# A two-norm block with a sorted mixture of experts on one core: norm sums in order of arrival, a rearranged last block, tie steps at half steps, and six units gathered ahead

## The chip, the cores and the metric

The kernel runs on one core of one Trainium2 chip. The metric is the device time of one execution in microseconds (us). Engines are named as in the profile: PE (TensorE), DVE (VectorE), ACT (ScalarE), POOL (GpSimd) and SP (SyncE, which only issues DMAs here). PEld is TensorE's weight load.

## What is computed

x has 2 sequences of 2048 rows of 128 channels (4096 rows in all). Six modulation vectors per sequence come from silu(c) @ wmod; ga and gb are kept away from zero.

```python
h = layernorm(x) * (1 + ca) + sa
x = x + ga * prefix_mean(h)            # row t gets the mean of rows 0..t of its sequence
h = layernorm(x) * (1 + cb) + sb
x = x + gb * ffn(h)
def ffn(h):                            # 8 experts, hidden width 512
    scores = softmax(h @ gate.T).T     # 8 x 4096
    vals, idx = top_k(scores.reshape(-1), 8192)   # over all experts and rows together
    out = sum over the chosen (expert, row) of val * (gelu(h[row] @ W1[e] + b1[e]) @ W2[e] + b2[e])
    return out + gelu(h @ Ws1 + bs1) @ Ws2 + bs2
```

How many rows an expert gets is known only at run time.

## The kernel before, in words

The rows are cut into NB = 8 blocks of BLK = 512 rows (four tiles of 128 each), and the five engines each run their own hand-written program, held together by counting semaphores. There are three stages.

**Norm stage.** For block j, `stats1(j)` on DVE takes mean and variance of the four tiles of x, `rstd(0, j)` on POOL makes 1/sqrt(var + eps) of it by a power (lines 730 to 741), `norm1(j)` on ACT (two tiles) and DVE (two tiles) normalizes, `turn_x(j)` on PE transposes the normalized tiles (semaphore pe_t1) and x itself (pe_t2), `prefix(j)` on DVE scans along the rows (line 434) and adds (lines 442, 448), `turn_x2(j)` on PE transposes back, `keep_x2(j)` on ACT stores. Then the second norm: `stats2(j)` on DVE, `rstd(1, j)` on POOL, `norm2(j)` on ACT (line 284), `turn_xn2(j)` on PE, `affine2(j)` on ACT (line 292), `logits(j)` (line 855) and `turn_h2(j)` on PE, `rows_out(j)` on ACT, and an SP store of the rows to a scratch tensor in HBM. In DVE's turn j stand norm1(j+1), prefix(j), stats2(j-1), stats1(j+3). In POOL's turn j stand rstd(1, j-1), then rstd(0, j+2). PE's turn j is turn_x(j+1), turn_xn2(j-2), turn_x2(j), logits(j-2), turn_h2(j-2); ACT's is norm1(j+1), norm2(j-2), rows_out(j-3), affine2(j-2), keep_x2(j). `softmax(part)` on DVE with `expo(part)` on ACT turns the logits into scores, part 0 for blocks 0 to 6 and part 1 for block 7.

**Shared stage, steps 0 to 31.** Step s holds `up(s)` (line 892) and `down(s-2)` (line 916) on PE, each 128x512 in float32, with `gelu(s)` on ACT between: the shared expert, four steps a block. `close(b)` (PE transposes, DVE adds X2, line 538, SP stores `out`) ends block b, four steps after its last up. Beside it a search of 30 bits finds the 8192nd largest score, one bit in each half step from half step 3 to 32 (`bit`). Then five tie steps sort out equal scores and make the counts of each expert: `ties(0)` at step 17 (masks), `ties(1)` at 18 (line 554), `ties(2)` at 19, `ties(3)` at 20 (line 570), `ties(4)` at 21 (PE transposes, line 948, then STC, `idx_mask(0)`, the units' experts EIDI, `idx_mm(0)`, `idx_count(0)`). Rows chosen for an expert are cut into units of up to 512 rows; between 16 and 23 units are in use (USED, 18 with this input). The list of rows of a unit comes from `idx_mask(v)` (DVE), `idx_mm(v)` (PE) and `idx_count(v)` (DVE, lines 646 to 655, which ends with IDXB and v_idx). Units 1 and 2 have theirs in steps 22 to 24.

**Unit stage, from step UNIT1 = 32.** Unit v has four steps, c = 0 to 3. PE runs in each step `up` (line 898), then what stands at that c, then `down` of two steps earlier. At c = 1 stand `xt(v+1)` (the transposes of the gathered rows of unit v+1, which wait for its gather to land) and `idx_mm(v+3)`; at c = 3 stands `yt(v-1)` (transposes of the result of unit v-1). So in PE's order yt(u) of unit u stands behind xt(u+2). DVE's `yo(u)` (line 689) scales the rows of yt(u) by their gates into YO, which has two buffers, and POOL scatters them:

```python
# before, POOL, in unit v's step c == 3
if 0 <= v - 1 < NU: scatter(v - 1)      # waits: yo(v-1) done, scatter(v-2) landed
if v + 3 < NU:      gather(v + 3)       # 4 indirect DMAs (line 766)
```

A scatter is four indirect DMAs that add to `out` (line 779). scatter(0) also waits until all of `out` from the shared stage has been stored. Gathers 0, 1 and 2 are issued before the unit stage; gather(3) and scatter(0) follow in it. gather(v) waits for v_idx of its unit, and for a free buffer of XG (XR = 5 of them). Units from UMIN = 16 on stand in a branch that skips them when they are not in use.

Of the kernel before, what the change touches and what calls it, by code (L numbers as in the profile page):

```python
# [32 lines left out]
XR = 5  # L33
# [7 lines left out]
TIE0 = max(BIT_AT) // 2 + 1  # L41
GS0 = NC * NB
UNIT1 = max(GS0, TIE0 + 8)
XT_STEP = UNIT1 - 1 - TIE0
# [3 lines left out]
ld_wu0 ld_wu1 ld_wu2 ld_wu3 ld_xg0 ld_xg1 ld_xg2 ld_xg3 ld_xg4  # L48
# [4 lines left out]
v_cols v_mod v_gbd v_st v_ag1 v_ag2 v_xn v_ct v_mt v_x2 v_sub v_sc v_tk v_cnt v_cand v_mask v_tie v_sel v_out  # L53
# [13 lines left out]
def adaln_moe(nc, x, gw, w1, b1, w2, b2, ws1, bs1, ws2, bs2, c_in, wmod, consts, ucon, icon, inv, out):  # L67
    rows_dram = nc.dram_tensor("rows_scratch", [S + NPAD, ROW], F32, kind="Internal").ap()

    with ExitStack() as ctx:  # L70
# [99 lines left out]
        TOKA = (NB - 1) * NT  # L170
# [12 lines left out]
        def sync(eng):  # L183
# [49 lines left out]
            for s in range(NSTEP):  # L233
                g = on_step(s - LAG - 2)
                if g is not None and g < GS0 and g % NC == NC - 1:
                    b = g // NC
# [4 lines left out]
                if s == TIE0 + 5:  # L241
# [10 lines left out]
        def scalar(eng):  # L252
# [54 lines left out]
            for j in range(NB + 2):  # L307
                if j + 1 < NB:
                    norm1(j + 1)
                if j >= 2:  # L310
                    norm2(j - 2)
                if j == 2:
# [50 lines left out]
            for s in range(NSTEP):  # L363
# [7 lines left out]
                if s == TIE0 + 4:  # L371
# [4 lines left out]
                if s == TIE0 + XT_STEP:  # L376
# [12 lines left out]
        def vector(eng):  # L389
# [33 lines left out]

            def prefix(b):
# [43 lines left out]
            def softmax(part):  # L468
# [3 lines left out]
                logits = LG[:, 0:TOKA * E] if part == 0 else RB[0][:, 0:NT * E]  # L472
# [4 lines left out]
                eng.wait_ge(M["pe_lg"], NB - 1 + part)  # L477
                k = step("v_tk", eng.tensor_reduce(mx, logits, AX_X, ALU.max))
                eng.wait_ge(M["v_tk"], k)
                eng.tensor_tensor(ex, logits, mx.unsqueeze(2).to_broadcast([P, n, E]),  # L480
                                  ALU.subtract).then_inc(M["v_sub"], 1)
# [14 lines left out]
            for j in range(NB):  # L496
# [43 lines left out]
            def ties(s):  # L540
                TF = T_I.bitcast(F32)
                ones = ONES[:, 0:1].to_broadcast([P, 256])
                if s == 0:
# [7 lines left out]
                elif s == 1:  # L551
# [8 lines left out]
                elif s == 2:  # L560
# [5 lines left out]
                elif s == 3:  # L566
# [32 lines left out]
                elif s == 4:  # L599
# [15 lines left out]
                elif s == 5:
                    idx_mask(1)
                elif s == 6:
                    idx_mask(2)
                    idx_count(1)
                elif s == 7:  # L620
                    idx_count(2)
# [70 lines left out]

            eng.wait_ge(M["v_sc"], 2)
            count(0)
            for s in range(NSTEP):
                if 2 * s in BIT_AT:
                    bit(BIT_AT[2 * s])
                g = on_step(s - LAG - 2)
                if g is not None and g < GS0 and g % NC == NC - 1:
                    close(g // NC)  # L700
                if 0 <= s - TIE0 <= XT_STEP:
                    ties(s - TIE0)
                if 2 * s + 1 in BIT_AT:
                    bit(BIT_AT[2 * s + 1])
                if s == TIE0 + XT_STEP:
# [369 lines left out]
```

## Time and profile before

| | us |
|---|---|
| median of 3 timed runs | 405.81 (405.25 to 410.68) |
| the profiled execution | 403.75 |
| its span in the trace | 402.0 |
| busy: PE / DVE / ACT / POOL | 297.1 / 168.1 / 138.1 / 209.7 |
| DMA | 35.96 MB, 89 GB/s on average |

A row of the timeline reads: start, duration, engine, line, operation, what is written <- what is read, shape, and, in brackets, how long the engine had been idle and what it had waited for. Several equal instructions in a row are merged (x4). Line numbers are those of the kernel printed above. R is one of the big SBUF and PSUM tensors whose names begin with R (the gathered rows among them), R1b the PSUM bank of the result transposes, XW holds x and later the experts' weights.

### The profile page before, as it was taken

Reading aid. Unit: us, or ns where it says so; the run is one execution under the profiler, and the core shown is the slowest. Engines: PE = TensorE matmul, PEld = TensorE weight load, DVE = VectorE, ACT = ScalarE, POOL = GpSimd, SP = SyncE. Lnnn points to the kernel's source line nnn. Section 1 sums busy time; section 2 is a strip of 40 time slices with the busy share of each in tenths; the row PEclk is TensorE's granted clock in tenths of the full one; section 3 lists DMA queues with packets and bytes.
Section 4 is the critical chain, followed back from the end, with each engine's and each line's share of the span. In section 5 each row is a group of like instructions: output and inputs, shape, how many; then the busy total and the mean of one; then the engine's idle time right before and its main releaser. Section 6 shows DMA issues by size and latency. Waiting matters only on the chain.

```text
span 402.0 us, 4835 instructions
## 1 busy us (share of the span) xinstructions
PE 297.1 (74%) x1158; PEld 162.7 (40%) x1158; DVE 168.1 (42%) x774; ACT 138.1 (34%) x228; POOL 209.7 (52%) x216
## 2 busy tenths in 40 slices
PE   1647667799999699998776977679786897669500
PEld 1536657653334344544332543335343344234200
DVE  2777748247775860244344213442144323211200
ACT  2135546743334235433233333233232333233200
POOL 2333443100000065037878788787888788786662
PEclk9998665569999999999899889898899989898955
DMA  8907200230000095044455554555445555342331
GB/s 231 294 2 201 62 27 30 68 48 0 27 28 27 26 277 147 28 127 87 76 118 126 105 102 82 115 126 106 100 82 119 125 103 104 74 73 27 30 34 13
DMA packets 49886, 35.96 MB, mean 89 GB/s; under 512 B 7816, under 2 KB 44479, under 8 KB 49855
## 3 DMA queue, kind: packets, MB, share of 16 engines
q0 software_dynamic: 13824, 14.46, 21.1%
q1 hardware_dynamic: 35792, 20.73, 18.5%
q10 hardware_dynamic: 238, 0.42, 0.4%
q8 instruction: 12, 0.20, 0.2%
q14 instruction: 20, 0.16, 0.1%
HBM read 23.65 MB, written 11.94 MB: 89 GB/s over the span
## 4 chain that ended last, share of the span: by engine, by line
POOL 34%; PE 23%; issue 17%; DMA 11%; DVE 11%; ACT 1%; SPq 1%; POOLq 0%; DVEq 0%; ACTq 0%
POOL out_dram L779 23%; POOL R L766 9%; PE Y L916 8%; DMA out_dram<-YO,IDXB 8%; PE U L892 7%; DVE R L434 2%; DMA XW<-in_L_attn_x_dram 2%; DVE ST L400 2%; PE U L898 2%; PE R1b L810 1%; DVE R L442 1%; DVE R L448 1%; PE R L810 1%; PE LG L855 1%; PE LG L922 1%
## 5 line engine op out<-in xcount | busy, mean ns | idle before, releaser
L779 POOL DMA_INDIRECT out_dram<-YO,IDXB x72 | 113.5, 1576 | 31.0 <-issue 20.7
L766 POOL DMA_INDIRECT R<-rows_scratch,IDXB x72 | 69.9, 971 | 105.5 <-DVE IDXB L655 68.9
L335 ACT ACTIVATE HF<-U,CB 128x512 f32<-128x512 f32 x72 | 49.5, 687 | 100.3 <-PE U L898 100.3
L916 PE MATMUL Y<-HF,XW 128*128 128x512 f32 x144 | 83.1, 664 | 0.0
L898 PE MATMUL U<-XT,XW 128*128 128x512 f32 x144 | 78.9, 631 | 0.7 <-issue 0.7
L689 DVE SCALAR_TENSOR_TENSOR YO<-R1b,GT,R 128x128 f32<-128x128 f32 x72 | 20.3, 344 | 122.4 <-PE R1b L810 122.4
L810 PE MATMUL R<-CST,R 128*128 128x128 f32 x104 | 21.5, 343 | 40.6 <-DMA R<-rows_scratch,IDXB 39.9
L898 PEld LDWEIGHTS U<-XT,XW 128*128 128x128 f32 x144 | 29.7, 208 | 39.6 <-issue 39.6
L810 PEld LDWEIGHTS R<-CST,R 128*128 128x128 f32 x104 | 15.0, 173 | 54.7 <-DMA R<-rows_scratch,IDXB 51.5
L892 PE MATMUL U<-H2F,WS 128*128 128x512 f32 x64 | 36.7, 663 | 0.0
L335 ACT ACTIVATE HF<-U,COL 128x512 f32<-128x512 f32 x32 | 22.0, 687 | 42.5 <-PE U L892 42.2
L916 PEld LDWEIGHTS Y<-HF,XW 128*128 128x128 f32 x144 | 27.2, 210 | 21.4 <-issue 21.4
L916 PE MATMUL Y<-HF,WS 128*128 128x512 f32 x64 | 34.7, 624 | 0.0
L735 POOL TENSOR_SCALAR VE<-MV 128x4 f32<-128x4 f32 x16 | 3.1, 194 | 45.2 <-DVE MV L403 44.8
L646 DVE TENSOR_SCALAR_CACHE_REDUCE GJ<-R,UC 128x128 f32<-128x128 f32 x72 | 25.1, 349 | 2.3 <-PE LG L971 0.4
L351 ACT ACTIVATE XT<-R 128x512 f32<-128x512 f32 x18 | 10.7, 595 | 41.9 <-PE R L810 41.9
L810 PE MATMUL U<-CST,R 128*128 128x128 f32 x32 | 8.9, 433 | 17.9 <-ACT R L270 15.8
L968 PE MATMUL R<-DQ,HM 128*128 128x128 f16 x144 | 15.4, 234 | 3.4 <-DVE HM L631 2.8
L738 POOL TENSOR_TENSOR RS<-VE,SM 128x4 f32<-128x4 f32 x16 | 16.2, 1015 | 0.0
L517 DVE TENSOR_SCALAR_CACHE_REDUCE TK<-SCT,TI 128x256 f32<-128x256 f32 x30 | 14.4, 479 | 1.1
L916 PEld LDWEIGHTS Y<-HF,WS 128*128 128x128 f32 x64 | 11.2, 194 | 8.7 <-issue 8.7
L810 PEld LDWEIGHTS U<-CST,R 128*128 128x128 f32 x32 | 5.9, 223 | 20.1 <-ACT R L270 17.7
(136 smaller groups left out, 357.6 us busy)
## 6 DMA issues: line engine op xcount, KB each, us to landing
XW<-in_L_ffn_W_dram SPq DMA_DIRECT2D x36, 256.0 KB, 3.1
XW<-in_L_attn_x_dram SPq DMA_DIRECT2D x8, 256.0 KB, 7.1
rows_scratch<-GBC SPq DMA_DIRECT2D x2, 1024.0 KB, 7.3
rows_scratch<-HT SPq DMA_DIRECT2D x8, 256.0 KB, 2.4
out_dram<-SHO SPq DMA_DIRECT2D x8, 256.0 KB, 2.3
R<-rows_scratch,IDXB POOLq DMA_INDIRECT x72, 2.8
out_dram<-YO,IDXB POOLq DMA_INDIRECT x72, 3.3
INV<-in_inv_dram SPq DMA_DIRECT2D x4, 256.0 KB, 6.4
```

The costliest lines, as they stand in the source:

```text
L335: eng.activation(HF[:, g % RING, :], UB[g % 2][:, :], ACT.Gelu_apprx_tanh, bias=bias).then_inc(M["a_gelu"], 1)
L517: eng.tensor_scalar(GT, SCT[:, :], C_I.bitcast(F32), None, ALU.is_ge, ALU.add, accum_out=CNT[:, i % 2:i % 2 + 1]).then_inc(M["v_cnt"], 1)
L646: eng.tensor_scalar(GJ[:, :], bank[:, s * P:(s + 1) * P], SIG[:, i:i + 1], None, ALU.is_le, ALU.add, accum_out=c0[:, s:s + 1]).then_inc(M[ ...
L689: m = eng.scalar_tensor_tensor(YO[:, k, t, :], RB[1][:, t * P:(t + 1) * P], GT4[:, k, t:t + 1], XG[:, r, t, D + E:ROW], ALU.mult, ALU.mult)
L738: eng.tensor_tensor(RS[:, k, b, 0, :], VE[:, k, b, :], NHALF, ALU.pow).then_inc(M["g_pw" + q], 1)
L766: eng.indirect_dma_start(XG[:, v % XR, s, :], None, rows_dram, bass.IndirectOffsetOnAxis(ap=IDXB[:, v, s:s + 1], axis=0)).then_inc(M[f"ld_ ...
L779: eng.indirect_dma_start(out, bass.IndirectOffsetOnAxis(ap=IDXB[:, v, s:s + 1], axis=0), YO[:, v % 2, s, :], None, compute_op=ALU.add).the ...
L810: m = eng.transpose(bank[:, t * P:(t + 1) * P], src(t), IDENT)
L892: eng.matmul(bank[:, :], WS[:, c * P:(c + 1) * P], H2F[:, u * BLK:(u + 1) * BLK], start=True, stop=True).then_inc(M["pe_up"], 1)
L898: eng.matmul(bank[:, :], WU[:, v % WR, c * P:(c + 1) * P], XT[:, v % 2, :], start=True, stop=True).then_inc(M["pe_up"], 1)
L916: eng.matmul(bank[:, :], down_weights(g), HF[:, g % RING, :], start=c == 0, stop=c == NC - 1).then_inc(M["pe_dn"], 1)
L968: eng.matmul(bank[:, s * P:(s + 1) * P], HM[:, v % 2, ch, s * P:(s + 1) * P], DQ[:, ch, :], start=ch == 0, stop=ch == 1)
```

## The change

- POOL's order in the norm stage: turn j is now rstd(1, j-1), then rstd(0, j+3), from j = 0 on.
- The last blocks: turn 7 of PE and ACT puts turn_x2(7) and keep_x2(7) first; norm2 of block 7 moves from ACT to DVE (`norm2_last`); turn_h2 and rows_out of blocks 5, 6 and 7 move behind logits(7); softmax part 0 covers blocks 0 to 4 only, in two halves, part 1 the other three, whose logits go to another PSUM bank (YB[0]).
- Tie steps are placed by half steps (H0 = 33): ties 0 at half step 33, 1 and 2 together at 34, 3 at 37, 4 at 42, idx_mm(0) and idx_count(0) at 43. close(3) moves from step 19 to 22.
- Six units (0 to 5) have their row lists made in the shared stage (masks at half steps 44, 47, 50, 53, 56; mm one, count two half steps later) and are gathered before scatter(0). In the unit stage lists are made for v+6 instead of v+3. XR is 8.
- POOL in the unit stage: scatter(v), then three gather DMAs (not four), until the lead over the scatters has shrunk, then four:

```diff
-XR = 5
+XR = 8
+AHEAD = 6
...
-TIE0 = max(BIT_AT) // 2 + 1
+H0 = max(BIT_AT) + 1
-UNIT1 = max(GS0, TIE0 + 8)
+UNIT1 = GS0
+K_TIE, K_CUM, K_DQ, K_IDX = 1, 4, 9, 10
+MASK_AT = {K_IDX - 2 + 3 * v: v for v in range(1, AHEAD)}
+EID_STEP = (H0 + K_IDX) // 2 + 1
+CLOSE_AT = {NC * b + NC - 1 + LAG + 2: b for b in range(NB)}
+CLOSE_AT[22] = CLOSE_AT.pop(19)
+PART0 = 5
+PER_GAP = 3
+def gathered(v):
+    return min(max(NT * AHEAD + PER_GAP * (v + 1), NT * (v + 4)), NT * NU)
...
 # ACT
-            for j in range(NB + 2):
+            for j in range(NB):
...
+                if j == NB - 1:
+                    keep_x2(j)
...
+            norm2(NB - 2)
+            expo(0)
+            affine2(NB - 2)
+            affine2(NB - 1)
             expo(1)
+            for b in range(NB - 3, NB):
+                rows_out(b)
...
 # DVE
+            def norm2_last():
+                b = NB - 1
+                eng.wait_ge(M["g_rs2"], NB)
+                eng.wait_ge(M["v_ag2"], NB)
+                eng.wait_ge(M["pe_t4"], NB - 2)
+                for t in range(NT):
+                    m = eng.tensor_scalar(XN2[:, b % 2, t, :], X2[:, b, t * P:(t + 1) * P], MV[:, 1, b, t, 0:1],
+                                          RS[:, 1, b, 0, t:t + 1], ALU.subtract, ALU.mult)
+                m.then_inc(M["v_xn2"], 1)
...
+            softmax(0, 0)
             stats2(NB - 1)
...
-            softmax(0)
-            softmax(1)
+            norm2_last()
+            softmax(0, 1)
+            softmax(1, 0)
+            softmax(1, 1)
...
 # DVE, unit stage
-                        if v + 3 < NU:
-                            idx_mask(v + 3)
+                        if v + AHEAD < NU:
+                            idx_mask(v + AHEAD)
...
 # POOL
-            for j in range(1, NB + 1):
-                rstd(1, j - 1)
-                if j + 2 < NB:
-                    rstd(0, j + 2)
+            for j in range(NB + 1):
+                if j:
+                    rstd(1, j - 1)
+                if j + 3 < NB:
+                    rstd(0, j + 3)
...
-            for s in range(NSTEP):
...
-                v, c = (s - UNIT1) // NC, (s - UNIT1) % NC
-                if v >= 0 and c == 3:
-                    if 0 <= v - 1 < NU:
-                        scatter(v - 1)
-                    if v + 3 < NU:
-                        gather(v + 3)
+            for q in range(gathered(-1)):
+                gather(q // NT, q % NT)
+            eng.wait_ge(M["v_used"], 1)
+            used = eng.value_load(USED[0:1, 0:1], min_val=UMIN, max_val=NU)
+            for v in range(NU):
+                scatter(v)
+                for q in range(gathered(v - 1), gathered(v)):
+                    gather(q // NT, q % NT)
...
 # PE, after its turns
+            turn_xn2(NB - 2)
+            logits(NB - 2)
+            turn_xn2(NB - 1)
+            logits(NB - 1)
+            for b in range(NB - 3, NB):
+                turn_h2(b)
...
+            def half_step(h):
+                if h in BIT_AT:
+                    bit(BIT_AT[h])
+                elif h >= H0:
+                    ties(h - H0)
...
-                        if v + 3 < NU:
-                            idx_mm(v + 3)
+                        if v + AHEAD < NU:
+                            idx_mm(v + AHEAD)
```

## Rows read from the trace of the kernel before

**Rows 1.** The page's chain by engine, and its costliest POOL groups.
```profile
POOL 34%; PE 23%; issue 17%; DMA 11%; DVE 11%; ACT 1%; SPq 1%; POOLq 0%; DVEq 0%; ACTq 0%
...
L779 POOL DMA_INDIRECT out_dram<-YO,IDXB x72 | 113.5, 1576 | 31.0 <-issue 20.7
L766 POOL DMA_INDIRECT R<-rows_scratch,IDXB x72 | 69.9, 971 | 105.5 <-DVE IDXB L655 68.9
```

**Rows 2.** Timeline of POOL and DVE over one turn of the norm stage.
```profile
36.02 0.60 DVE L420 TENSOR_SCALAR R<-XW,MV,RS 128x128 f32<-128x128 f32 x2 [2.45 <-POOL RS L741]
...
41.37 0.38 DVE L403 BATCH_NORM_AGGREGATE MV<-ST 128x2 f32<-128x6 f32 x4
...
43.96 0.20 POOL L741 TENSOR_TENSOR RS<-NM,RS 128x4 f32<-128x4 f32 x1
44.20 0.60 DVE L420 TENSOR_SCALAR R<-XW,MV,RS 128x128 f32<-128x128 f32 x2 [2.45 <-POOL RS L741]
```

**Rows 3.** Busy time by stretch: PE, PEld, DVE, ACT, POOL, PEclk, DMA share, GB/s.
```profile
61.10:69.30 8.20, 6.95 (x30) 6.08 (x31) 7.67 (x22) 5.79 (x13) 1.96 (x5) 0.50 0.10 33
```

**Rows 4.** Timeline, PE in the norm stage: four transposes, eight logits matmuls.
```profile
62.33 1.06 PE L810 MATMUL Y<-CST,XW 128*128 128x128 f32 x4
...
63.19 1.06 PE L810 MATMUL R1b<-CST,R 128*128 128x128 f32 x4
...
65.11 1.88 PE L855 MATMUL LG<-COL,H2F 128*128 128x8 f32 x8
```

**Rows 5.** Timeline, from the last block's scan to the shared stage's first matmul.
```profile
64.97 1.25 DVE L434 TENSOR_TENSOR_SCAN R<-CST,R,U 128x512 f32<-128x512 f32 x1
...
75.23 1.63 ACT L284 ACTIVATE R<-X,RS 128x128 f32<-128x128 f32 x4
...
83.88 3.62 PE L892 MATMUL U<-H2F,WS 128*128 128x512 f32 x4
```

**Rows 6.** Timeline of DVE, tie steps and the first unit's row list.
```profile
128.46 0.16 DVE L554 TENSOR_SCALAR SM<-LG 128x1 f32<-128x1 f32 x1 [3.27 <-PE R L938]
...
139.18 0.34 DVE L646 TENSOR_SCALAR_CACHE_REDUCE GJ<-R,UC 128x128 f32<-128x128 f32 x1
...
141.33 0.16 DVE L655 TENSOR_TENSOR IDXB<-CNB 128x4 uint32<-128x4 f32 x1
```

**Rows 7.** Timeline of PE: step 22 after the tie steps, unit 0's first up.
```profile
138.92 1.80 PE L892 MATMUL U<-H2F,WS 128*128 128x512 f32 x2
...
162.74 1.10 PE L898 MATMUL U<-XT,XW 128*128 128x512 f32 x2 [0.73 <-issue]
```

**Rows 8.** Timeline of POOL: scatter(0), the gather behind it, scatter(1).
```profile
181.50 1.62 POOL L779 DMA_INDIRECT out_dram<-YO,IDXB  x1 [2.98 <-DVE YO L689]
...
189.07 1.02 POOL L766 DMA_INDIRECT R<-rows_scratch,IDXB  x1 [0.30 <-issue]
...
194.18 1.62 POOL L779 DMA_INDIRECT out_dram<-YO,IDXB  x1 [0.30 <-issue]
```

**Rows 9.** The chain that ended last, landing of scatter(0)'s last DMA.
```profile
187.21 4.37 DMA out_dram<-YO,IDXB
```

**Rows 10.** Busy time by stretch (columns as in rows 3), one unit of the unit stage.
```profile
206.80:219.50 12.70, 8.70 (x40) 4.46 (x40) 5.48 (x28) 3.92 (x6) 10.23 (x9) 1.00 0.52 105
```

**Rows 11.** Timeline: the last gather, what it releases, and scatters 15 and 17.
```profile
357.24 0.95 POOL L766 DMA_INDIRECT R<-rows_scratch,IDXB  x1 [0.30 <-issue]
358.49 1.62 POOL L779 DMA_INDIRECT out_dram<-YO,IDXB  x1 [0.30 <-issue]
...
360.08 0.66 PE L810 MATMUL R<-CST,R 128*128 128x128 f32 x4 [3.06 <-DMA R<-rows_scratch,IDXB]
...
366.41 1.13 DVE L689 SCALAR_TENSOR_TENSOR YO<-R1b,GT,R 128x128 f32<-128x128 f32 x4 [10.63 <-PE R1b L810]
...
368.22 1.56 POOL L779 DMA_INDIRECT out_dram<-YO,IDXB  x1 [2.49 <-DVE YO L689]
...
387.33 1.56 POOL L779 DMA_INDIRECT out_dram<-YO,IDXB  x1 [2.42 <-DMA out_dram<-YO,IDXB]
```

More of the change, by code:

```diff
@@ L466, in modulation, with softmax @@
                 eng.tensor_scalar(GBS, GG[:, 1, :], B2[:, 8:9], None, ALU.mult).then_inc(M["v_mod"], 1)
-            def softmax(part):
+            def softmax(part, half):
                 t0, t1 = (0, TOKA) if part == 0 else (TOKA, NB * NT)
                 n = t1 - t0
-                logits = LG[:, 0:TOKA * E] if part == 0 else RB[0][:, 0:NT * E]
+                logits = LG[:, 0:n * E] if part == 0 else YB[0][:, 0:n * E]
                 logits = logits.rearrange("p (t e) -> p t e", e=E)
@@ L476, in softmax @@
                 mx, sm, rc = (RED[:, i, t0:t1] for i in range(3))
[L477 to L481, printed above, removed]
+                if half == 0:
+                    eng.wait_ge(M["pe_lg"], NB if part else PART0)
+                    k = step("v_tk", eng.tensor_reduce(mx, logits, AX_X, ALU.max))
+                    eng.wait_ge(M["v_tk"], k)
+                    eng.tensor_tensor(ex, logits, mx.unsqueeze(2).to_broadcast([P, n, E]),
+                                      ALU.subtract).then_inc(M["v_sub"], 1)
+                    return
                 eng.wait_ge(M["a_exp"], part + 1)
@@ L614, in ties @@
                                       E8.unsqueeze(1).to_broadcast([P, NU, E]), ALU.is_equal).then_inc(M["v_oh"], 1)
[L615 to L621, printed above, removed]
+                if k in MASK_AT:
+                    idx_mask(MASK_AT[k])
+                elif k - 2 in MASK_AT:
+                    idx_count(MASK_AT[k - 2])
             def idx_mask(v):
@@ L695, in vector @@
             for s in range(NSTEP):
[L696 to L705, printed above, removed]
+                half_step(2 * s)
+                if s in CLOSE_AT:
+                    close(CLOSE_AT[s])
+                half_step(2 * s + 1)
+                if s == UNIT1 - 1:
                     eng.wait_ge(M["v_used"], 1)
@@ L866, in tensor @@
             turn_x(0)
-            for j in range(NB + 2):
+            for j in range(NB):
                 if j + 1 < NB:
                     turn_x(j + 1)
+                if j == NB - 1:
+                    turn_x2(j)
                 if j == 2:
@@ L879, in tensor @@
                     logits(j - 2)
-                    turn_h2(j - 2)
+                    if j < NB - 1:
+                        turn_h2(j - 2)
+            turn_xn2(NB - 2)
[4 more added lines that the diff above has]
+                turn_h2(b)
             def up(g):
@@ L951, in ties @@
                     m.then_inc(M["pe_dq"], 1)
+                elif k == K_IDX:
                     idx_mm(0)
[L953 to L956 removed]
+                elif k - 1 in MASK_AT:
+                    idx_mm(MASK_AT[k - 1])
             def idx_mm(v):
@@ L991, in yt, with half_step @@
                     transposes(RB[1], lambda t: YE[:, v % 2, t * P:(t + 1) * P]).then_inc(M["pe_yt"], 1)
+            def half_step(h):
+                if h in BIT_AT:
+                    bit(BIT_AT[h])
+                elif h >= H0:
+                    ties(h - H0)
             for s in range(NSTEP):
@@ L997, in tensor @@
                         up(g)
-                if 2 * s in BIT_AT:
-                    bit(BIT_AT[2 * s])
+                half_step(2 * s)
                 g = on_step(s - LAG)
@@ L1002, in tensor @@
                     down(g)
-                g = on_step(s - LAG - 2)
-                if g is not None and g < GS0 and g % NC == NC - 1:
-                    close(g // NC)
-                if 0 <= s - TIE0 <= XT_STEP:
-                    ties(s - TIE0)
-                if 2 * s + 1 in BIT_AT:
-                    bit(BIT_AT[2 * s + 1])
-                if s == TIE0 + XT_STEP:
+                if s in CLOSE_AT:
+                    close(CLOSE_AT[s])
+                half_step(2 * s + 1)
+                if s == UNIT1 - 1:
                     eng.wait_ge(M["v_used"], 1)
```

104 lines of the change are left out of this document (45 added, 59 removed).

## The prediction, made before the changed kernel was run

> **What bounds the kernel now.** I read the chain that ended last first. POOL holds 34% of it, nearly all in two lines, the scatter DMAs (72 of 1.58 us) and the gather DMAs (72 of 0.97 us) [rows 1]: 72 is 18 units of 4. Then the timeline by stage.
>
> Norm stage, up to 83.9 us. DVE begins a turn every 44.20 - 36.02 = 8.18 us, but its own work of a turn ends at 41.37 + 0.38 = 41.75, after 5.73. The rest it waits for POOL, whose last result comes at 43.96 + 0.20 [rows 2]. POOL computes rstd(1, j-2) and then rstd(0, j+1), and norm1(j+1) needs the second at once. PE is the next in line: 6.95 us busy in a turn at a granted clock of 0.50, the 1.2 GHz level [rows 3]. Counted by starts, four transposes take 0.86 and the logits of a block about 1.8 [rows 4], so five groups and the logits make 6.1.
>
> Shared stage, 83.9 to 162.7 [rows 5, 7]: the bit search sets the pace up to step 16, then the tie steps stall PE.
>
> Unit stage: scatter(0) starts at 181.50, scatter(1) at 194.18, and POOL's gaps in it are 0.30 [rows 8]. A period is 12.65: four scatters 7.55 (189.07 - 181.50), four gathers 5.1. PE's work for a unit fits easily: 8.70 at full clock [rows 10]. Scatter(14) is at 358.49; scatter 15 at 368.22 and 17 at 387.33 come 9.73 and twice 9.55 apart, as no gathers stand between and the landing of the one before is awaited [rows 11]. So from scatter(0) to scatter(17) it is 205.83 now, and 14.7 more to the end of the span.
>
> **Norm stage, new.** POOL now makes rstd(0, j+3) right after its sums, a whole turn before they are needed, so DVE doesn't wait for it. A turn then lasts 5.73 if DVE bounds it and 6.1 if PE does at the low clock. I take 6.1. ACT is no bound: norm2's four tiles wait for rstd(1) and end some 5 us after the previous turn_x2, in time for PE. The Trainium skill (TensorE: Matmul & The Clock Gate, Part 4: PE-mode transpose) says that transposes don't count as busy for the clock gate. By that rule PE stays at the low level however dense the turns; the clock of 0.50 over a turn that is 85% busy agrees, and it is why 6.1 rather than 5.73.
> Four turns (2 to 5) shrink by 8.18 - 6.1 = 2.1 each, and turn 2 starts 2.45 earlier, since that is the wait in front of it: 8.3 + 2.4 = 10.7. The last scan moves from 65.0 to 54.3.
>
> The way of the last block: from that scan it is 83.88 - 64.97 = 18.9 now [rows 5]. New, from 54.3: the x2 transposes of block 7 end at 58.2, its stored copy at 58.9, its sums at 60.4, its rstd at 62.1, DVE's norm (4 tiles, 1.15) at 63.2. But PE comes to it late: norm2(6) waits for rstd(1, 6) until 60.3 and ends at 62.2, the table load and exponent of softmax part 0 now stand before affine2(6) (1.7), which ends at 64.7; logits(6) to 66.5, transposes of 7 to 67.4, affine2(7) 68.3, logits(7) 70.1. Then three turn_h2, each waiting for the rows_out before it as they share a bank: 4.0, to 74.1. That is 19.8, 0.9 longer than before: what the move of norm2 saves is given back by two more turn_h2 that used to lie between. So up(0) starts at 74.1 instead of 83.9: **-9.8**. Ends: if turns stay at 7.3 (PE's waits add to its 6.1), -5; if DVE bounds and the last way shortens by 2, -14.
>
> **Tie steps and six lists.** Up to step 16 nothing changes. In the times of before: DVE stood 3.27 before tie 1 [rows 6]; placed at half step 34 it starts at 125.9 instead of 128.46, tie 3 at 129.1, and PE finds its inputs at 133.1 with no stall of note. idx_count(0) ends at 138.1 instead of 141.5, and up(22) starts at 135.4 instead of 138.92, at the high clock (the 1.80 there is the low level [rows 7]). But three more lists are then made here. A list costs DVE 0.6 (mask) + 0.75 (waiting for PE) + 2.3 (141.33 + 0.16 - 139.18, the count [rows 6]) = 3.7, in order, for 1.5 steps of PE's 1.72 and 0.65 for idx_mm. DVE is the slower one, and PE stalls on the masks 1.4 + 0.7 + 0.35 + 0.4 + 1.9 = 4.7. I come to up(32) at 163.8 instead of 162.74 [rows 7]: **+1.1**. Ends: -3 (no stalls), +4 (PE falls to the low clock in them).
> POOL's 24 gathers of 1.26 run from 138.2 to 168.4, before yo(0) at some 182 of the same clock of times: hidden; were they late, each would cost 1.26. Close(3) at step 22 holds up SP's loads of weights, queued behind it, until about 140, as now: nothing. Scatter(0) so starts at 181.5 - 9.8 + 1.1 = 172.8.
>
> **Unit stage, POOL's own work.** `gathered(v)` gives 27, 30, ... 60 for v = 0 to 11, then 64, 68, 72. So there are 12 gaps of three gathers, 12.65 - 1.25 = 11.40, three of four, 12.65, and two of 9.55: 136.8 + 38.0 + 19.1 = 193.9 against 205.8: **-12.0**. The landing of a scatter stays covered: 4.37 after its last DMA's start [rows 9], and the next scatter starts 1.86 + 3.8 = 5.66 after it.
>
> **Unit stage, the new wait.** This decides. yo(v) needs yt(v), and in PE's order yt(v) stands behind xt(v+2), so scatter(v) needs gather(v+2) landed and what follows it. From the start of the last DMA of gather(17), 357.24: landed and PE starts at 360.08, yo(15) starts 366.41, ends 367.54, scatter(15) at 368.22 [rows 11]: 10.98; from scatter(0)'s row the last hop can be 0.3 rather than 0.7, so I take L = 10.8.
> Before, POOL had gathered v+3 units when it came to scatter(v): gather(v+2) lay a whole period of 12.65 back, more than 10.8, and nothing waited. New, `gathered(v-1)` is max(24 + 3v, 4v + 12), while scatter(v) needs 4v + 12: the lead is 12 - v DMAs and is gone at v = 12. Up to v = 9 the needed DMA lies before scatter(v-1) (1.25 + 11.4 = 12.7 back). For v = 10 it is the first of the gap's three (3.85 before scatter(v) could start), for 11 the second (2.52), for 12 to 15 the last (1.25). Units 18 and on are skipped, so 16 and 17 don't wait. Waits: 6.95 + 8.28 + 4 x 9.55 = **+53.4**. In that stretch a period is 22 us; POOL's gathers are queued behind the waiting scatter, PE waits for the gathers: a ring of POOL, DMA, PE, DVE that was two periods long and is one now. Ends for L: 9.5 if PE ran at the high clock (the rows after 360.08 are partly low), 13.1 if all at the low one.
>
> **Sum.** -9.8 + 1.1 - 12.0 + 53.4 = +32.7. The profiled execution took 403.75 (span 402.0): 436.4. The median is 2.06 above it: 438.
>
> **Rivals.**
> A, the other side: POOL stays bound by its own work to the end. Its place is scatter 10 to 15, its price the absent 53.4: 405.8 - 9.8 + 1.1 - 12.0 = 385. For it: PE needs only 8.70 a unit and POOL's gaps are 0.30, so the trace of before shows no such wait but the 2.49 at scatter(15) [rows 11]. It holds if the way from a gather to yo is under 3.85 us; the row shows 10.3, of which the landing alone is 2.84. 0.05.
> B: after rests of 10 us PE runs the whole chain at the low clock: five pieces of 0.9 to 1.7 make 8.6 instead of 6.3, six waits of 2.3 more: 452. For it: the rest before 360.08 was only 3.06, now it is longer. Against: the low stretch there ended before the chain did. 0.13.
> C: the norm stage's new POOL order doesn't do what it says, as another wait (ACT's norm2, PE) holds the turn near 8: no gain there, 448. For it: PE is 85% busy already. Against: DVE's wait is named POOL each turn. 0.09.
> D: PE returns to the high clock quickly, L = 9.5: 6 x 1.3 less, 430. 0.12.
> E: part of the waits is eaten by a lead I don't see, landing within 2%. 0.03.
> The forecast has 0.58.
>
> **How the numbers follow.** About 2% is what a measurement of this kernel can tell from no change. A is faster, 0.05; E the same, 0.03; all others slower, 0.92. The range must reach from D's 430, with some 4 more of norm-stage gain, to B's edge: 426 to 450.
>
> **What would show it.** Norm turns of about 6.1 with no POOL wait before line 420's instruction; up(0) near 74; idx_count(0) ended near 128; scatter(0) near 173 with POOL idle before it; scatter to scatter 11.4 up to the tenth; then about 18, 20, 21 and three of 22, with POOL waiting some 7 to 10 us each for DVE's YO, and PE waiting some 10 us for gathered rows; last two 9.55. It is wrong if the scatter spacing stays 11.4 to 12.7 to the end: then yt(v) doesn't depend on gather(v+2) as I read it.

## The result, and the profile after

The changed kernel takes **452.52 us** (median of 3 runs, 452.35 to 454.48) against 405.81: ratio 1.1139, 95% interval 1.1025 to 1.1254, slower. The prediction was 438. The profiled execution took 452.5 too; its span is 450.7 against 402.0, the granted clock 0.847 against 0.873.

The page after: the chain by engine and the two POOL groups that answer to [rows 1].

```profile
POOL 28%; issue 25%; PE 23%; DVE 10%; DMA 6%; another core or an unknown queue 3%; ACT 2%; SPq 1%; POOLq 0%; DVEq 0%; ACTq 0%
...
L813 POOL DMA_INDIRECT out_dram<-YO,IDXB x72 | 113.9, 1582 | 100.7 <-DVE YO L720 76.7
L800 POOL DMA_INDIRECT R<-rows_scratch,IDXB x72 | 70.7, 982 | 97.4 <-DVE IDXB L686 76.4
```

POOL's work is the same (113.9 and 70.7 us), but it now idles 76.7 us for DVE's YO, 20.4 of them before scatter(0) and 56.4 before scatters 10 to 15, and "issue", which was 17%, is 25%. The timeline of POOL shows where: the first DMA of scatter 0, 1, 9, 10, 12 and 15 to 17.

```profile
184.97 1.62 POOL L813 DMA_INDIRECT out_dram<-YO,IDXB  x1 [20.37 <-DVE YO L720]
...
196.44 1.64 POOL L813 DMA_INDIRECT out_dram<-YO,IDXB  x1 [0.30 <-issue]
...
288.06 1.62 POOL L813 DMA_INDIRECT out_dram<-YO,IDXB  x1 [0.30 <-issue]
...
306.93 1.62 POOL L813 DMA_INDIRECT out_dram<-YO,IDXB  x1 [7.79 <-DVE YO L720]
...
347.42 1.62 POOL L813 DMA_INDIRECT out_dram<-YO,IDXB  x1 [9.64 <-DVE YO L720]
...
414.82 1.62 POOL L813 DMA_INDIRECT out_dram<-YO,IDXB  x1 [10.44 <-DVE YO L720]
...
424.44 1.55 POOL L813 DMA_INDIRECT out_dram<-YO,IDXB  x1 [2.38 <-DMA out_dram<-YO,IDXB]
...
433.98 1.55 POOL L813 DMA_INDIRECT out_dram<-YO,IDXB  x1 [2.41 <-DMA out_dram<-YO,IDXB]
```

A period is 11.5 up to scatter(9), where it was 12.65 [rows 8]. Scatters 10 to 15 wait 7.79, 8.61, 9.64, 10.55, 9.33 and 10.44, and come 19 to 23 us apart. The last two are 9.6 apart.

Timeline of DVE and PE from the norm stage's scans to the first up, answering to [rows 2, 5]; the last line is unit 0's first up, answering to [rows 7].

```profile
36.88 1.21 DVE L463 TENSOR_TENSOR_SCAN R<-CST,U 128x512 f32<-128x512 f32 x1
...
42.44 1.27 DVE L463 TENSOR_TENSOR_SCAN R<-CST,R,U 128x512 f32<-128x512 f32 x1
...
50.84 1.25 DVE L463 TENSOR_TENSOR_SCAN R<-CST,R,U 128x512 f32<-128x512 f32 x1
...
70.79 3.25 PE L930 MATMUL U<-H2F,WS 128*128 128x512 f32 x4
...
166.31 1.10 PE L936 MATMUL U<-XT,XW 128*128 128x512 f32 x2 [2.54 <-issue]
```

A turn is 42.44 - 36.88 = 5.56 instead of 8.18. up(0) starts at 70.8, 13.1 earlier. But from up(0) to up(32) it is 95.5 instead of 78.9. The timelines of DVE and ACT there show a wait that the profile can't name:

```profile
137.41 0.35 DVE L677 TENSOR_SCALAR_CACHE_REDUCE GJ<-R,UC 128x128 f32<-128x128 f32 x1 [6.76 <-remote]
137.49 0.69 ACT L354 ACTIVATE HF<-U,COL 128x512 f32<-128x512 f32 x1 [6.53 <-remote]
```

and in the chain that ended last it stands twice:

```profile
130.64 6.74 another core or an unknown queue
...
144.49 7.05 another core or an unknown queue
```

On one core there is no other core. PE's records show idx_mm(2) over at 131.50 and nothing else in its way, yet DVE's count, which waits for PE's semaphore, goes on at 137.41, and so does gelu on ACT, which waits for a later matmul's. The trace also keeps the times of the semaphore updates: that of idx_mm(2) came at 137.38, and three later ones of PE with it, until 137.51. So PE's updates came late, and several at once. I call these waits the stalls. The profile of before has nothing of the kind.

**The difference by pieces** (predicted; first measurement; the repetition e5 below, which has no such stalls; us):

| piece | predicted | first | e5 |
|---|---|---|---|
| up to up(0) | -9.8 | -13.1 | -13.5 |
| up(0) to up(32) | +1.1 | +16.7 | +3.7 |
| POOL's own work, scatter(0) to (17) | -12.0 | -11.4 | -11.5 |
| waits of scatters 10 to 15 | +53.4 | +54.6 | +57.4 |
| scatter(17) to the end | 0 | +2.0 | +2.1 |
| up(32) to scatter(0) | 0 | -0.1 | -0.1 |
| sum | +32.7 | +48.7 | +38.1 |

The waits are the six idle times less the 0.30 that POOL spends before any DMA. Own work is what is left from scatter(0) to scatter(17). All pieces are of the profiled executions.

### The profile page after: what moved, and what is told of

Read it like the earlier page. It is cut to its first block, busy times and chain, and to the rows that moved or that the text cites. A ratio compares the mean times of both kernels' runs of the same rounds, so it can differ in the third digit from the quotient of the medians.

```text
span 450.7 us, 4864 instructions
## 1 busy us (share of the span) xinstructions
PE 293.1 (65%) x1158; PEld 156.7 (35%) x1158; DVE 167.7 (37%) x778; ACT 135.6 (30%) x224; POOL 211.3 (47%) x216
## 4 chain that ended last, share of the span: by engine, by line
POOL 28%; issue 25%; PE 23%; DVE 10%; DMA 6%; another core or an unknown queue 3%; ACT 2%; SPq 1%; POOLq 0%; DVEq 0%; ACTq 0%
POOL out_dram L813 21%; PE Y L955 7%; POOL R L800 7%; PE U L930 5%; PE R L836 2%; PE U L936 2%; DMA R<-rows_scratch,IDXB 2%; DMA XW<-in_L_attn_x_dram 2%; PE R1b L836 2%; DVE ST L419 1%; DMA out_dram<-YO,IDXB 1%; DVE R L463 1%; DVE GJ L677 1%; PE R L1006 1%
## 5 line engine op out<-in xcount | busy, mean ns | idle before, releaser
L813 POOL DMA_INDIRECT out_dram<-YO,IDXB x72 | 113.9, 1582 | 100.7 <-DVE YO L720 76.7
L800 POOL DMA_INDIRECT R<-rows_scratch,IDXB x72 | 70.7, 982 | 97.4 <-DVE IDXB L686 76.4
L936 PE MATMUL U<-XT,XW 128*128 128x512 f32 x144 | 77.5, 621 | 2.5 <-issue 2.5
L955 PEld LDWEIGHTS Y<-HF,XW 128*128 128x128 f32 x144 | 27.4, 212 | 20.4 <-issue 20.4
L1006 PEld LDWEIGHTS R<-DQ,HM 128*128 128x128 f16 x144 | 9.6, 100 | 27.9 <-DVE HM L662 22.4
L930 PEld LDWEIGHTS U<-H2F,WS 128*128 128x128 f32 x64 | 11.5, 210 | 6.1 <-issue 5.7
```

Source lines behind the costliest of these rows:

```text
L800: eng.indirect_dma_start(XG[:, v % XR, s, :], None, rows_dram, bass.IndirectOffsetOnAxis(ap=IDXB[:, v, s:s + 1], axis=0)).then_inc(M[f"ld_ ...
L813: eng.indirect_dma_start(out, bass.IndirectOffsetOnAxis(ap=IDXB[:, v, s:s + 1], axis=0), YO[:, v % 2, s, :], None, compute_op=ALU.add).the ...
L930: eng.matmul(bank[:, :], WS[:, c * P:(c + 1) * P], H2F[:, u * BLK:(u + 1) * BLK], start=True, stop=True).then_inc(M["pe_up"], 1)
L936: eng.matmul(bank[:, :], WU[:, v % WR, c * P:(c + 1) * P], XT[:, v % 2, :], start=True, stop=True).then_inc(M["pe_up"], 1)
L955: eng.matmul(bank[:, :], down_weights(g), HF[:, g % RING, :], start=c == 0, stop=c == NC - 1).then_inc(M["pe_dn"], 1)
L1006: eng.matmul(bank[:, s * P:(s + 1) * P], HM[:, v % 2, ch, s * P:(s + 1) * P], DQ[:, ch, :], start=ch == 0, stop=ch == 1)
```

## The experiments

They ran on four chips: e1 to e4, e5 to e8, and e16 to e18 on one each, where no late update showed; e9 to e15 on a fourth, where it did. I call that the trait of a chip. Which chip the first measurement used isn't on record. Each is held against the kernel before on its own chip (403.2 to 404.8).

**e1, one unit of lead given back.**

```
-    return min(max(NT * AHEAD + PER_GAP * (v + 1), NT * (v + 4)), NT * NU)
+    return min(max(NT * AHEAD + PER_GAP * (v + 1), NT * (v + 5)), NT * NU)
```

> The changed kernel with the gathers held one unit further ahead (the floor of the schedule is v+5 units instead of v+4, as the order of before had it). My theory: the waits of scatter(10) to scatter(15), 7.8 to 10.6 us each, 56.4 in sum, come only from the lost unit of lead, so they vanish; scatter(0) to scatter(17) becomes 8 x 11.4 + 6 x 12.65 + 3 x 9.55 = 195.8 instead of 249.0, and the time 452.5 - 53 = 399. The shared stage is untouched, so scatter(0) stays near 185. Rival (the ring of POOL, DMA, PE and DVE is slow for another reason, as the clock of PE): the waits stay, 440 or more.

387.06 us, ratio 0.9581 (0.9556 to 0.9606): faster than before. Timeline of POOL, scatters 0, 8, 9 and 14:

```profile
172.25 1.62 POOL L813 DMA_INDIRECT out_dram<-YO,IDXB  x1 [16.21 <-DVE YO L720]
...
263.47 1.62 POOL L813 DMA_INDIRECT out_dram<-YO,IDXB  x1 [0.30 <-issue]
...
276.14 1.61 POOL L813 DMA_INDIRECT out_dram<-YO,IDXB  x1 [0.30 <-issue]
...
339.26 1.62 POOL L813 DMA_INDIRECT out_dram<-YO,IDXB  x1 [0.30 <-issue]
```

The six waits are gone: the period is 11.4 while gaps hold three gathers and 12.65 after (276.14 - 263.47 = 12.67). From scatter(0) to (17) it is 196.0, expected 195.8. What I had not expected is scatter(0) at 172.25, 12.7 earlier than in the first measurement, from the same instructions: the stalls were absent. This is where the prediction had put it (172.8).

**e2 to e4: pauses, late gathers, late weight loads**, each on top of e1.

```
e2   eng.wait_ge(M["v_idx"], v + 1 if v >= AHEAD else min(v + 2, AHEAD))
e3   eng.wait_ge(M["v_idx"], max(v + 1, AHEAD))
e4   if s == UNIT1 - 2:      (was: if s == EID_STEP, on SP)
```

> As e1_lead5, and POOL waits for list v+2 before it gathers unit v (v below 6), so two units are not gathered back to back while lists are still made. Theory G (a run of eight gathers without a pause holds back PE's semaphore updates in the shared stage, the stalls of 6.8 and 7.1 us at 130.6 and 144.5): no stall over 4 us, up(32) at 158 or earlier instead of 166.3, scatter(0) near 176, time near 391. Rival P (the stalls have to do with the memory layout or with PE's own instructions): stalls as before, time as e1_lead5, 399.

> As e1_lead5, but no gather before the sixth list is made, so the shared stage runs without gathers. If gathers cause the stalls (G), they vanish: the sixth list is ready near 153 instead of 164, up(32) near 154, but the 24 gathers of 1.26 us then stand before scatter(0): first gather 153, the last ends at 183, scatter(0) near 183 to 184, time near 398. If they are not the cause (P): sixth list at 164, gathers to 194, scatter(0) near 195, time near 409.

> As e1_lead5, but SP issues the weight loads of the first four units (2 MB) some nine steps later, just before the unit stage. If the loads' traffic beside the gathers causes the stalls (W), the first stall (6.8 us at 130.6) goes or moves to where the loads now are, and scatter(0) comes some 6 us earlier, time near 393. If not, the stalls stay where they are and the time is 399; the loads still land before up(32), within 1 us.

386.94, 393.19 and 387.42 us. As their base e1 had no stalls, e2 and e4 tell nothing of them; e4 says that the time of the loads is free. Nor did e2 pause anything: it moved POOL's first gather to 129.35, and from there the 24 gathers went through to 159.3 with 0.30 between them. e3 is under both expectations, since both were counted with the stalls in: the sixth list was ready near 148, the 24 gathers ran from 148.4 to 178.5 without a pause, and scatter(0) came right behind them at 178.78. On this chip such a run did not stall PE, and neither did e1's, 24 gathers from 125.96 to 156.04 beside five idx_mm.

**e5, the changed kernel again, unchanged.**

> The changed kernel once more, not a letter different, beside its neighbours e6 to e8. e1_lead5, whose stages up to scatter(0) are the same instructions, had no stall in the shared stage and scatter(0) at 172.25. Theory C (the three stalls, 6.8, 7.1 and 2.9 us, belong to the executions or the chip of the first measurement and not to the program): this run has no late PE semaphore update, scatter(0) near 172.3, and the time 172.3 + 249.0 - 2 + 18 = 437 to 440. Rival M (they belong to the program with the floor v+4, by something in its POOL code or the loading of it): stalls as in the first measurement, 452.

440.96 us (439.82 to 441.89), ratio 1.0911 (1.0868 to 1.0954), 1 us over what theory C had. Timeline of POOL, scatters 0, 9, 10, 13 and 17:

```profile
171.59 1.62 POOL L813 DMA_INDIRECT out_dram<-YO,IDXB  x1 [16.22 <-DVE YO L720]
...
274.45 1.62 POOL L813 DMA_INDIRECT out_dram<-YO,IDXB  x1 [0.30 <-issue]
...
294.75 1.62 POOL L813 DMA_INDIRECT out_dram<-YO,IDXB  x1 [9.22 <-DVE YO L720]
...
359.28 1.62 POOL L813 DMA_INDIRECT out_dram<-YO,IDXB  x1 [10.73 <-DVE YO L720]
...
423.30 1.55 POOL L813 DMA_INDIRECT out_dram<-YO,IDXB  x1 [2.55 <-DMA out_dram<-YO,IDXB]
```

So 12 us of the first measurement belong to something that doesn't come with the program; e12 below brings it back on another chip. The same trace shows the new chain before scatter(13), in a timeline of all engines:

```profile
347.60 0.95 POOL L800 DMA_INDIRECT R<-rows_scratch,IDXB  x1 [0.30 <-issue]
350.38 1.11 PE L836 MATMUL R<-CST,R 128*128 128x128 f32 x4 [12.26 <-DMA R<-rows_scratch,IDXB]
...
353.00 1.91 PE L936 MATMUL U<-XT,XW 128*128 128x512 f32 x2
...
357.18 0.60 PE L836 MATMUL R1b<-CST,YE 128*128 128x128 f32 x4
...
357.87 1.13 DVE L720 SCALAR_TENSOR_TENSOR YO<-R1b,GT,R 128x128 f32<-128x128 f32 x4 [21.10 <-PE R1b L836]
```

Gather(15)'s last DMA starts at 347.60, its rows are there at 350.38, PE transposes them after 12.3 us of rest, works off four matmuls at 1.9 a pair (the low level; 1.02 at the high one), comes to yt(13) at 357.18, DVE's YO starts at 357.87, and scatter(13) at 359.28. L is 11.7 here, where I took 10.8.

**e6, POOL's old order in the norm stage**, on top of e1.

```
+            for j in range(1, NB + 1):
+                rstd(1, j - 1)
+                if j + 2 < NB:
+                    rstd(0, j + 2)
```

> e1_lead5 with POOL's old order in the norm stage (rstd(1, j-1), then rstd(0, j+2)), everything else as changed. Theory: the norm turns 2 to 5 go back from 5.6 to about 8.2 us, so up(0) comes some 10 to 13 us later and the time is 387 + 12 = 399. Rival (the shorter way of the last block carries the gain, not POOL's order): less than 4 us lost, 391.

400.79 us, ratio 0.9932 (0.9912 to 0.9952): 13.7 over e1, which ran on another chip. The timeline of DVE and PE has the scans 8.17 apart again, and the first up 14.1 later than e1's 70.71:

```profile
36.44 1.27 DVE L463 TENSOR_TENSOR_SCAN R<-CST,R,U 128x512 f32<-128x512 f32 x1
...
44.61 1.22 DVE L463 TENSOR_TENSOR_SCAN R<-CST,U 128x512 f32<-128x512 f32 x1
...
64.87 1.25 DVE L463 TENSOR_TENSOR_SCAN R<-CST,R,U 128x512 f32<-128x512 f32 x1
...
84.81 3.56 PE L929 MATMUL U<-H2F,WS 128*128 128x512 f32 x4
```

From the last scan to up(0) it is 19.94 here and 19.94 in e1 (50.77 to 70.71), against 18.91 before [rows 5]: the new way of the last block costs 1.0; POOL's order carries the whole gain.

**e7, the lead taken from the kernel before.**

```
-                    if v + 3 < NU:
-                        gather(v + 3)
+                    if v >= 1 and v + 2 < NU:
+                        gather(v + 2)
```

> The kernel before with one thing moved: gather(v+2) instead of gather(v+3) behind scatter(v-1), so that unit v+2 is gathered right before scatter(v) and the lead is gone from the first unit on. Theory (scatter(v) can't start before gather(v+2) has landed and PE, ACT and DVE have worked off what follows it, L = 10.8 to 11.8): POOL waits 9.6 to 10.6 us before each of scatter(1) to scatter(15), the period is 22 to 23 instead of 12.65, and the time 403.6 + 15 x 10 = 554 (range 545 to 562). Rival (the waits in the changed kernel come from its six lists or its ring of eight, not from the lead): time within 10 us of before, 404 to 414.

569.04 us, ratio 1.4096, above my range of 545 to 562: 165 us slower by moving each gather one place. Of the scatters 1 to 15, the timeline shows 1 and 10:

```profile
203.60 1.62 POOL L779 DMA_INDIRECT out_dram<-YO,IDXB  x1 [10.48 <-DVE YO L689]
...
417.54 1.62 POOL L779 DMA_INDIRECT out_dram<-YO,IDXB  x1 [11.49 <-DVE YO L689]
```

The waits settle at 11.5, 1 to 2 over my expectation, and that is the miss; the period is 23.9. The lead alone makes the waits, without six lists, a larger ring, or anything else of the change.

**e8, yt before xt on PE**, with the change's own schedule of gathers.

```
 (PE, at c == 3)   yt(v - 1), then xt(v + 1)      (was: xt(v + 1) at c == 1)
 (ACT, at c == 3)  copy_x(v + 1)                  (was: at c == 1)
```

> The changed kernel with its own schedule of gathers (floor v+4), but xt(v+1) on PE and copy_x(v+1) on ACT moved two steps later, behind yt(v-1). Theory (the wait exists only because yt(v) stands behind xt(v+2) in PE's order): scatter(v) now needs only gather(v+1), which lies a period back, so no wait of POOL over 2 us before scatter 10 to 15, the period there is 12.65, and the time within 5 us of e1_lead5, 387 to 392 (if the shared stage has its stalls, 12 more). Rival (the chain runs through the buffers, whatever PE's order is): waits of 8 to 10 us, 435 or more.

388.34 us, ratio 0.9614 (0.9582 to 0.9646). Scatters 10 to 15 wait 0.30, 0.30, 0.46, 0.31, 0.30 and 0.30; scatter(16) waits 5.55 for DVE's YO, where e1's waits 2.40 for a landing. So the chain is one of order on PE, as the prediction said: yt(v) stood behind xt(v+2).

**e9 to e12, on the fourth chip.** e9 is e1 with AHEAD = 3. e10 is e1 with one more unit before scatter(0), e11 the same with AHEAD = 7 and XR = 9, e12 the changed kernel unchanged.

```
e10, e11   return min(max(NT * (AHEAD + 1) + PER_GAP * (v + 1), NT * (v + 5)), NT * NU)
```

> e1_lead5 with three lists ahead instead of six (AHEAD 3), so the half steps and the norm stage stay as changed, but only three lists are made in the shared stage and 16 gathers stand before scatter(0). Theory: the 3.7 us by which the changed shared stage is longer than before's (82.5 against 78.9 from up(0) to up(32)) are the three more lists; without them it is 77 to 79, scatter(0) comes near 167, every gap of POOL is 12.65 up to scatter(14), 205.8 in all, and the time 167 + 206 + 19 = 392. Rival (the half steps cost the 3.7): the stage stays at 82 to 83 and the time is 396 to 397.

> e1_lead5, but POOL gathers the seventh unit too before scatter(0): its list is made at 164.2 anyway and POOL is idle from 156 to 172. Theory (POOL's own work after scatter(0) bounds the rest, and what is put into its idle time is gained in full): four gathers of 1.25 less behind scatter(0), 387.1 - 5.0 = 382. Rival (PE or the chain per unit is near its bound at 11.4 already): less than 2 us gained, 385 to 387.

> As e10_seventh_unit with seven lists ahead (AHEAD 7) and a ring of nine, so eight units stand gathered before scatter(0). Theory: ten us of gathers less than e1_lead5 behind scatter(0), against 1.5 to 2.5 us more in the shared stage for the seventh list: 379 to 380. Rival (the gathers of the eighth unit run into scatter(0), as its list comes with unit 0 at about 165): 382 to 384.

> The changed kernel a third time, unchanged, for the stalls of the first measurement (6.8, 7.1 and 2.9 us between 130 and 166). If they come and go with the chip or the placing of a program, either 440 (none, as in e5_after_again) or 452 (as the first time) can come; if 440 again, the first measurement is the odd one and its 12 us are no part of the change.

394.11, 393.91, 393.81 and 452.62 us. The changed kernel is at its first time again, and all four have the first stall (DVE waits 5.9 to 6.6 us, until 137.0 to 137.3); e10, e11 and e12 have the second one as well, and e10 and e11 a third. e10's scatter(0) is at 185.06, 12.8 behind e1's, and from there its POOL needs 191.1, 4.9 less than e1's 196.0: the seventh unit gives its 5 us, and the stalls take 12.8. Of e10 and e11 there is no measurement without stalls. e9 leaves open what it was for: from up(0) to up(32) it takes 79.6 with one stall in it, against e1's 82.9 with none, so three of the six lists cost at least 3.3 (the chips differ); how much more, its stall hides.

**e13 to e15, what the stalls are tied to.** All have e10's schedule; e13 is e10 again, e14 adds the wait of e3, e15 the later loads of e4.

> e10_seventh_unit once more. Where PE's late updates are absent (as in e1 and e5): scatter(0) near 172 and 382, my expectation of e10 unchanged. Where they are there (as in e10, e12): scatter(0) near 185 and 394. This is also the base that e14 and e15 are held against, as they run on the same chip.

> e13 with no gather before the sixth list is made. Theory G (PE's updates are held back only while POOL issues a long run of gathers): no late update before the sixth list, which is ready at 147 in any case; 28 gathers of 1.26 then run to 183, scatter(0) near 184 and 393 to 394 with or without the trait. Rival L (the weight loads or something else on that chip hold them): where the trait is there, the sixth list comes at 152 or later and the time is 399 or more.

> e13 with the first weight loads (2 MB) some nine steps later. Theory G: nothing changes, within 1 us of e13, with its stalls at 131 and 145 where e13 has them. Rival L: where e13 has the stalls, the first one (6.6 us from 130.5) is gone or moved to where the loads now are, and the time is 4 to 7 us under e13.

394.61, 403.52 and 395.75 us. In e15 the weight loads, which e13 issues from 129.6 to 138.5, stand at 152.2 to 161.0. Timeline of DVE, the counts of the third and the fourth list:

```profile
133.14 0.35 DVE L677 TENSOR_SCALAR_CACHE_REDUCE GJ<-R,UC 128x128 f32<-128x128 f32 x1 [2.35 <-PE LG L1009]
...
143.13 0.35 DVE L677 TENSOR_SCALAR_CACHE_REDUCE GJ<-R,UC 128x128 f32<-128x128 f32 x1 [7.05 <-remote]
```

The long stall is one list later than in e13, where the third list's count waited 6.57 us before 138.55. In updates: idx_mm(2)'s came 1.5 us late in e15 and 5.7 in e13, idx_mm(3)'s 6.2 late with no load under way. So a stall needs no weight loads, and the time is 1.1 over e13's and not 4 to 7 under: rival L falls. But "nothing changes" doesn't hold either; the loads may lengthen a delay, which nothing here tries by itself. e14 is the telling one. Timeline of DVE, the third and the sixth list, and then the wait:

```profile
133.51 0.16 DVE L686 TENSOR_TENSOR IDXB<-CNB 128x4 uint32<-128x4 f32 x1
...
146.78 0.16 DVE L686 TENSOR_TENSOR IDXB<-CNB 128x4 uint32<-128x4 f32 x1
...
181.31 0.69 DVE L572 TENSOR_TENSOR SHO<-R1b,X 128x512 f32<-128x512 f32 x1 [25.50 <-remote]
```

Without gathers beside it, the shared stage runs as on the other chips (list six at 146.78; e1's at 147.21). Then POOL issues 24 gathers without a pause, from 147.25 to 177.2, and the timeline of PE shows when the trouble starts:

```profile
162.47 0.28 PE L1006 MATMUL R<-DQ,HM 128*128 128x128 f16 x2
...
163.07 0.19 PE L1009 MATMUL LG<-IC,HM 128*128 128x1 f16 x2
163.12 1.10 PE L936 MATMUL U<-XT,XW 128*128 128x512 f32 x2
...
166.22 1.02 PE L955 MATMUL Y<-HF,XW 128*128 128x512 f32 x2
181.91 2.08 PE L936 MATMUL U<-XT,XW 128*128 128x512 f32 x2 [14.67 <-ACT HF L354]
```

For the first 15 us of the run PE's updates are on time. Then comes idx_mm(6) at 162.47, 32 short float16 instructions, over at 163.26. Its update is recorded at 181.10, and those of the five groups behind it follow until 181.33, 4 us after the run. The seventh list comes at 184.2 by it, and the last four gathers with it, so e14 takes 403.5, where theory G had 393 to 394; rival L's later sixth list isn't there either. In the first measurement the first late one is idx_mm(2) at 130.70, in a run of eight gathers that began at 125.77, and the wait ends 1.5 us after the run.

**What the update times say of idx_mm.** A trace holds 18 idx_mm. In the twelve traces without the trait, that of before among them, every recorded update of theirs (213) came 0.01 us after the last matmul. In the eight with it (the first measurement and e9 to e15) the 23 idx_mm that had no indirect DMA of POOL within half a microsecond of their end were on time as well; of the 118 that had one, 76 were more than 0.1 us late. That isn't confined to long runs of gathers: in the unit stage, where scatters and gathers alternate, they were up to 2.0 us late, and POOL's own work took no longer by it. In e14 the idx_mm of the six lists, which have no gathers beside them, were on time, and so was what PE told in the first 15 us of the run, which have no idx_mm.

What this shows: with the trait, idx_mm without POOL's DMAs did nothing, 15 us of gathers without an idx_mm did nothing, and most late series begin where the two meet. Not all do: the third stall of the first measurement and of e10 (the update of xt, 1.8 and 2.2 us late) and the series in e15 from 157 on stand in a run of gathers, but behind an idx_mm that was itself on time or 0.8 us late. The last update of a long stall came 1 to 4 us after the run; in e15 some came while it still ran. No run takes idx_mm away with all else the same. How the one would hold up the other isn't shown, and neither is why one chip does this and three don't.

**e16 to e18.** One execution of the kernel before; e1 with POOL waiting for each of the first six units to land; and e1.

```
+                    if s == NT - 1 and v < AHEAD:
+                        eng.wait_ge(M[f"ld_xg{v}"], 64)
```

> The kernel before, unchanged, for one look at its shared stage on this chip. Its gathers come as a run of four (about 141 to 147) and a run of eight (148 to 158). If a run of over some 5 us is all that is needed, PE's updates are late between 154 and 159.5 where the trait is there, and up(32) comes 3 to 5 us later than on a chip without it; if such a run must also meet an idx_mm, nothing shows, as in the profile of before. Time 403.6 to 404.8.

> e1_lead5, but POOL waits for the landing of each of the first six units before it issues the next unit's gathers, so no run is longer than four. It costs six pauses of 2 to 2.5 us, which end at about 168, before scatter(0) at 172: nothing where the trait is absent, 387. Theory G2 (the run's length counts): no update over 2 us late and 386 to 389 on either kind of chip. Rival (any gather beside idx_mm): where e18 has stalls this has them too and is not more than 3 us under it.

> e1_lead5 once more, as the base of e17 on the same chip. 387 where PE's late updates are absent; 387 + 12 = 399 where they are there (scatter(0) near 185).

403.76, 389.32 and 386.85 us, on a chip without the trait, so e16 says nothing of what it was for. The remedy stays untried where it would be needed, and costs 2.5 here: the first pause was 5.9 us instead of 2 to 3, with the weight loads running beside it. e18 repeats e1 on a second chip: 0.9590 (0.9562 to 0.9619). It is the version to keep.

## Why the prediction was right or wrong

**What bounds the end: right.** The wait is in the place named (scatters 10 to 15), with the releaser named (DVE's YO), for the reason named. e1, e7 and e8 take it away and bring it back from three sides. Its size was +53.4 against 54.6 and 57.4. Within it, scatter(10) waited 7.5 to 8.9 (less the 0.30) instead of 6.95, and the later ones up to 10.4 instead of 9.55, as PE ran more of the chain at the low level after its rests: rival B's mechanism, with 1.2 and 4.0 of the 13.8 us that B gave it. B's case against itself was right: the low stretch ends before the chain does.

**Norm stage: right in kind, 3.3 short.** The step that failed is "I take 6.1", the turn bound by PE at the low clock. Turns were 5.6 long and the last of the four 4.4, which is DVE's own work (5.47 of 5.61 and 4.33 of 4.44 in the rows below); the last has one block less to take statistics of, which the wait for POOL had covered. The rule behind that choice was the Trainium skill's (TensorE: Matmul & The Clock Gate, Part 4: PE-mode transpose), that transposes don't count as busy. The denser turns don't bear it out. Busy time by stretch after (columns as in rows 3), the turns that begin at 31.27, 42.44 and 46.88:

```profile
31.27:36.88 5.61, 4.49 (x33) 3.39 (x32) 5.47 (x23) 4.45 (x10) 3.21 (x8) 0.92 1.07 278
...
42.44:46.88 4.44, 4.19 (x20) 3.29 (x21) 4.33 (x15) 3.35 (x7) 2.09 (x7) 0.62 0.21 61
46.88:50.84 3.96, 2.85 (x25) 2.49 (x25) 3.85 (x12) 3.13 (x9) 1.32 (x3) 1.00 0.01 2
```

The clock was 0.92 in one turn, 0.62 in another and 1.00 in the last, with nothing but transposes and logits on PE. And the turns don't follow it: in e1 the same four stretches last 5.61, 5.55, 4.44 and 3.96, at clocks of 1.00, 1.00, 0.99 and 0.58. So PE was the bound in none of them. The trace of before had the warning: beside two stretches at 0.50 it has

```profile
36.60:44.80 8.20, 5.09 (x28) 4.52 (x28) 5.61 (x23) 4.23 (x10) 3.10 (x8) 0.72 0.64 166
...
52.90:61.10 8.20, 5.37 (x28) 4.67 (x28) 4.47 (x15) 4.29 (x10) 3.10 (x8) 0.71 0.11 33
```

[rows 3] is also no turn of the middle: two scans, at 61.01 and 64.97, lie in it, hence its 6.95 of PE. By the end that the prediction named beside it, 5.73 a turn, the four turns give 9.8 instead of 8.3; the short last turn gives 1.3 more. The last block's way, +0.9 predicted, measured +1.0 (e6, e1).

**Shared stage: wrong on the first chip, near on the others.** The failed step is "Tie steps and six lists ... +1.1", with its range of -3 to +4. Where nothing disturbs, it was +3.7, inside that range. Its two halves part at up(22), in e5's timeline of PE:

```profile
122.49 1.10 PE L930 MATMUL U<-H2F,WS 128*128 128x512 f32 x2
...
152.91 1.09 PE L936 MATMUL U<-XT,XW 128*128 128x512 f32 x2 [0.73 <-issue]
```

Counted from up(0), up(22) came at 52.1 instead of 55.0, so the tie steps gave 2.9 where 3.5 was predicted; from up(22) to up(32) it took 30.4 instead of 23.8, so the three more lists cost 6.6 where 4.6 was: that part was sized too low. On the chip of the first measurement the term was +16.7. The step "POOL's 24 gathers ... before yo(0): hidden" failed there: POOL was hidden, but beside its gathers PE's messages to the others were held up. No row of before could warn of it: eight gathers in a row ran there as well, but that trace shows no sign of the trait: its updates of idx_mm are on time in the unit stage too, where those of the changed kernel's first trace are up to 1.5 us late. This term alone carried the time out of the range: with e5's +3.7 in its place the 452.5 would be 439.5.

**End of the span: 2.1 left out.** I took over the 14.7 behind scatter(17) unchanged. It is 16.7 to 16.8 in the first measurement, in e5 and in e1, and 14.7 in e16. A gather now has an If of its own, so more skipped branches stand there; that they are the cause is argued and was not tried.

**Sum.** On its chip, without the trait, e5's 440.96 stands against 403.6: +37.4, predicted +32 from median to median. That is nearer than the terms were: the norm stage was 3.7 better than predicted, the waits 4.0, the shared stage 2.6 and the end 2.1 worse, and these cancel in part. That scatter(0) came at 172.25 in e1, where it was predicted, is luck in the same way: the norm stage was shorter and the shared stage longer. The first measurement lies 16.0 over the 436.4 of the profiled execution; the 2.06 added for the median were not there, as the profiled execution took the median itself.

## What to carry to other kernels

When a producer's queue is thinned out, write down for each step how many of its DMAs lie between the one that the step needs and the step itself, and what stands before the needed instruction in every engine's order: one unit of lead was worth 165 us in e7, and one line gave 54 back in e1. A transfer that is hidden from the engines that compute can still be heard by them: idx_mm was put beside longer runs of indirect DMAs here, and in the first measurement and on one of the four chips since that cost 12 us. And where a time doesn't fit and the profile names no releaser, measure the same program on another chip before you explain it.

## What the runs showed of the hardware that I had not expected

- Chips differ by more than their run-to-run spread for one and the same program: 452.5 and 452.6 on two occasions, 441.0 on another chip, while the medians of the kernel before differ by 1.6 us at most between the four chips (403.2 to 404.8; the first measurement had 405.8, of three runs).
- On such a chip PE's semaphore updates came up to 17.8 us late (e14: idx_mm(6) over at 163.3, its update at 181.1). idx_mm's were late only with indirect DMAs of POOL beside them (76 of 118, and none of 23 without), and the last of a long stall came 1 to 4 us after the run of gathers. The stalled stretch also left PE at the low level: the pair of matmuls at 181.91 took 2.08.
- On the other chips runs of 24 gathers without a pause (e1, e3) stopped nothing, idx_mm beside them or not.
